# GpSimd's power for the next block's norm moved from slot 43 to slot 45, the normalisations of x from slots 45-48 to 46-49

## What is computed

```python
x = x + layernorm(attention(layernorm(x)))
x = x + layernorm(ffn(layernorm(x)))
```

## Time and profile before

| | us |
|---|---|
| median of 3 runs | 2466.63 (2465.53 to 2471.25) |
| the profiled execution, its own time | 2470.34 |
| its span, first to last instruction | 2468.6 |
| TensorE busy | 2360.2 (96% of the span) |
| VectorE busy | 1564.6 (63%) |
| ScalarE busy | 1399.9 (57%) |
| GpSimd busy | 659.3 (27%) |
| mean granted TensorE clock | 0.983 of 2.4 GHz |

### The profile page before, as it was taken

One profiled execution on the slowest core, in us unless ns is written; L12 is line 12 of the kernel. 1 busy time (PEld: TensorE's weight loads), 2 busy tenths in 40 slices (PEclk: granted clock), 3 DMA queues, 4 the chain that ended last, 5 costly groups with the idle time before them and its releaser, 6 DMA issues.

```text
span 2468.6 us, 38369 instructions
## 1 busy us (share of the span) xinstructions
PE 2360.2 (96%) x13020; PEld 1082.7 (44%) x13020; DVE 1564.6 (63%) x4343; ACT 1399.9 (57%) x3867; POOL 659.3 (27%) x923
## 2 busy tenths in 40 slices
PE   7589999999999999999999999999999999999988
PEld 3244444444444444444444444444443444444433
DVE  7857476665757657575665757656575765757542
ACT  4647456474755647466464755647466564755710
POOL 5412313122231312223132231312223132222312
PEclk9799999999999999999999999999999999999999
DMA  5010121201212020121201112020121202012000
GB/s 148 19 49 21 52 52 36 69 18 43 45 44 60 27 73 23 35 52 35 69 19 52 35 46 58 31 72 20 35 52 44 61 19 70 17 52 52 19 18 18
DMA packets 99523, 108.89 MB, mean 44 GB/s; under 512 B 22895, under 2 KB 73199, under 8 KB 99311
## 3 DMA queue, kind: packets, MB, share of 16 engines
q1 hardware_dynamic: 98462, 105.65, 16.1%
q10 hardware_dynamic: 864, 0.79, 0.1%
HBM read 38.49 MB, written 16.78 MB: 22 GB/s over the span
## 4 chain that ended last, share of the span: by engine, by line
PE 91%; DVE 4%; ACT 2%; POOL 2%; issue 1%; DMA 0%; ACTq 0%; POOLq 0%; DVEq 0%; SPq 0%
PE dense L376 65%; PE psO L579 7%; PE score L563 4%; PE psO L376 4%; PE low L546 3%; PE score L546 3%; DVE st_ln L826 1%; PE low L563 1%; POOL rs_ln L1188 1%; PE low L382 1%; PE low L471 1%; ACT arena L768 1%; PE score L471 1%; POOL arena L1321 1%; PE score L382 1%
## 5 line engine op out<-in xcount | busy, mean ns | idle before, releaser
L376 PE MATMUL dense<-arena,wgu 128*128 128x512 f16 x3872 | 920.1, 379 | 1.0 <-DVE arena L929 1.0
L376 PE MATMUL dense<-wdn,arena 128*128 128x512 f16 x2112 | 540.4, 382 | 2.6 <-POOL arena L1258 2.6
L376 PEld LDWEIGHTS dense<-arena,wgu 128*128 128x128 f16 x3872 | 369.5, 97 | 393.7 <-issue 7.6
L768 ACT ACTIVATE arena<-score 128x512 f32<-128x512 f32 (+3 forms) x720 | 300.2, 437 | 228.5 <-PE score L563 188.3
L1129 DVE CUSTOM_DVE_ANT_0 low<-low,mmax 128x128 f32<-128x128 f32 (+3 forms) x672 | 278.3, 435 | 229.8 <-PE low L546 226.9
L1258 POOL TENSOR_TENSOR arena<-late,arena 128x512 f16<-128x512 f32 x176 | 203.5, 1156 | 820.6 <-DVE arena L963 610.1
L684 ACT ACTIVATE low<-low,ncol 128x128 f32<-128x128 f32 (+3 forms) x672 | 299.8, 446 | 129.1 <-DVE ncol L1129 122.4
L684 ACT ACTIVATE score<-score,ncol 128x384 f32<-128x384 f32 x352 | 214.3, 609 | 139.9 <-DVE ncol L1129 139.6
L376 PEld LDWEIGHTS dense<-wdn,arena 128*128 128x128 f16 x2112 | 200.5, 98 | 185.7 <-issue 12.5
L1129 DVE CUSTOM_DVE_ANT_0 score<-score,mmax 128x384 f32<-128x384 f32 x352 | 214.3, 649 | 76.8 <-PE score L546 75.9
L1321 POOL TENSOR_SCALAR_AFFINE_SELECT arena<-arena 128x512 f32<-128x512 f32 x240 | 157.6, 657 | 279.0 <-ACT arena L768 278.9
(11 more groups left out here) (181 smaller groups left out, 2919.4 us busy)
## 6 DMA issues: line engine op xcount, KB each, us to landing
qst<-arena SPq DMA_DIRECT2D x384, 64.0 KB, 2.0
kst<-arena SPq DMA_DIRECT2D x186, 128.0 KB, 2.6
xin<-x SPq DMA_DIRECT2D x16, 1024.0 KB, 5.1
late<-x SPq DMA_DIRECT2D x64, 256.0 KB, 2.8
out<-late SPq DMA_DIRECT2D x64, 256.0 KB, 2.0
qst<-mrow SPq DMA_DIRECT2D x96, 8.0 KB, 1.9
wgu<-wo_t SPq DMA_DIRECT2D x1, 1024.0 KB, 13.0
wgu<-wq_down SPq DMA_DIRECT2D x1, 768.0 KB, 4.3
```

The lines of the kernel that those rows point to most:

```text
L376: ins = nc.tensor.matmul(dst, w, a, start=first and k == 0, stop=last and k == len(tt) - 1)
L768: nc.scalar.activation(prob_of(e // HG)[:, e % HG, 0:wide], st_bank(e)[:, 0:wide], ACT.Exp, scale=1.0 / S_SCORE).then_inc(sem["exp"], 1)
```

## The change

The power for the next block's norm is issued by GpSimd in slot 45 instead of slot 43, behind the place where a slot's mask stands and ahead of the feed-forward part's work of that slot. GpSimd's order becomes: mask 4 (42), mask 5 (44), power ln1 (45), power lo 0 (45), mask 6 (46), addition 0 (47), mask 7 (48). The four normalisations of x stand in slots 46 to 49 instead of 45 to 48, so that on VectorE the first comes behind the norm of output tile 0 and the fourth behind the moments of output tile 1. The moments of x stay in slot 43. No instruction is added or removed.

```diff
-LN1_SLOT = 43
+LN1_SLOT, LN1_POWER, LN1_NORM = 43, 45, 46
...
-                    if nxt and LN1_SLOT + 2 <= slot < LN1_SLOT + 2 + NT:
-                        i = slot - LN1_SLOT - 2
+                    if nxt and LN1_NORM <= slot < LN1_NORM + NT:
+                        i = slot - LN1_NORM
                         dve.wait_ge(sem["rs"], val("rs", t, n_ln1))
                         normalise("ln1", xin[:, i, :], xin[:, i, :], i).then_inc(sem["ln1"], 1)
...
                     for e in exp_tiles:
                         if e % HG == 1 and e > 1:
                             keep_causal(e // HG - 1)
+                    if nxt and slot == LN1_POWER:
+                        power(t, "ln1", n_y)
                     if ffn:
                         for m in range(MI):
                             if slot == up_done(m, 1) + 2:
...
                                 power(t, "lo", n_y + i + 1, i, i + 1)
-                    if nxt and slot == LN1_SLOT:
-                        power(t, "ln1", n_y)
```

## The result

The changed kernel takes 2435.27 us (median of 4 runs, 2434.26 to 2437.07), against 2468.94 for the kernel before (median of 4 runs, 2465.53 to 2474.2): a ratio of 0.9869, 95% interval 0.9856 to 0.9881. The forecast was 2436. The profiled execution took 2435.92 us with a span of 2434.2, so 34.4 us less than before on either count. That pair flatters the change: before and after were executed again beside the experiments, and there the kernel before took 2467.1 to 2467.4 (medians of 7 to 19 executions) and the changed one 2436.2, so the gain between medians is nearer 31 to 32 us.

What follows compares the result with a forecast made beforehand. TensorE is the bound, pausing for GpSimd's masks queued behind a norm power that waits for VectorE. 19.2 + 5.3 + 9.4 = 33.9 us off the profiled 2470.34 gives 2436, range 2430 to 2450.

Steps and rivals of the forecast that it cites:

- Mask 5 runs before values 5 is due: GpSimd, slot 44: causal mask of stage 5 ends 1.7 us before TensorE's probability-times-V products (values 5) want it; their wait goes.
- Mask 6 is late next: GpSimd, slot 46: stage-6 mask queued behind two powers; pause of 2.6 us becomes 1.3, gaining 1.37 us a block, 19.2 total.
- Mask 7 just fits: GpSimd, slot 48: stage-7 mask ends 0.16 us before TensorE wants values 7, so it costs nothing.
- rival 2: 8% chance: mask 7 becomes the wait, making values 7 0.9 us late in 14 blocks, 2448 us.
- rivals 3 to 5: In order: pause at values 6 hidden, 2418, 5%; VectorE's moments delayed, slower, 2474, 2%; little gained, 2449 to 2453, 3%.
- The normalisations of x cost nothing: VectorE, slots 46 to 49: the later normalisations cost nothing; should their cover fail, at most 0.5 us a block.
- Block 0: First block, mask 5 behind a weight unit: values 5 3.9 us sooner, with clock 5.3 us taken (bounds 3.9 and 5.9).
- Clock: Blocks 1 to 14: the halved pause brings fewer TensorE clock drops; 9.4 of 11.4 us lost is won back.
- rival 1: 20% chance: clock goes on falling at values 6; 2445 us if half the blocks drop as now, 2454 if all 14.
- The first case's own range: Main case, 62%: 2431 to 2441 us, from 0.95 to 1.37 us a block and clock losses 0 to 4.
- The total wait at L579: TensorE's total wait at the probability-times-V products for GpSimd's mask: some 22 us, the longest near 1.7.

Runs made afterwards that it cites:

- Experiment 3: Changed kernel with the normalisations of x starting in slot 45 again, the power left in slot 45: 2441.53 us, run again 2442.19 us.
- experiment 5: Changed kernel plus one or two unused extra GpSimd powers behind ln1's power in blocks 1 to 14: 2443.26 us with one, 2466.23 us with two.
- experiment 6: Changed kernel with powers ln1 and lo 0 in slot 46 behind mask 6, addition 0 in slot 48 behind mask 7: 2418.87 us.
- experiment 1: Changed kernel with power ln1 back in slot 43, normalisations left in slots 46 to 49: 2467.63 us, ratio 1.0006 to the kernel before.
- experiment 4: Changed kernel with power and normalisations of blocks 1 to 14 put back, change kept in block 0 alone: 2462.61 us, beside 2467.09 for the kernel before.

## Why the prediction was right

The forecast was 2436 and the time 2435.27. Counted from the medians the forecast was a gain of 30.2, against 31 to 32 measured. By its steps:

- *Mask 5 runs before values 5 is due.* Right. It runs 0.47 after values 4 for 0.85 (0.46 and 0.84 had been taken from the last block), and the wait at values 5 is gone. The mask was to be stretched beside VectorE's split, by what the Trainium skill has in SBUF — State Buffer, "Who interferes with whom", and nothing else was; the trace agrees: 0.85 for the mask beside the usual 0.63, and VectorE's L970 takes 0.69 with the mask beside it and without.
- *Mask 6 is late next.* Right: values 6 6.75 after values 4 was forecast, 6.72 is in the trace, so 1.41 and not 1.37 a block, 19.7 us. Both unstretched durations, L1022's 0.16 and the power's 0.55, came as the last block had them. Experiment 3 shows the second is owed to the later normalisations, the one part of the change that isn't the order on GpSimd; experiments 5 and 6 show that this queue alone sets values 6.
- *Mask 7 just fits.* Right, with 0.14 to spare where 0.16 was worked out; rival 2 did not come. Nor did rivals 3 to 5: values 6 does wait, L1022 starts 5.28 after values 4 (5.26 before), and the 14 pauses are shorter by 1.41 with no clock lost in them.
- *The normalisations of x cost nothing.* Right; with them alone the time is that of the kernel before (experiment 1).
- *Block 0.* 5.3 forecast, 5.3 in the traces, 4.5 with that block alone changed (experiment 4). The number is right by a path that was partly wrong. The sum had 3.9 at values 5 and 1.4 for the clock; the trace has 2.8 at values 5 and 2.5 behind it. The low clock came already at values 4 (1.51 there), so the transposes L403 took 1.06 and not 0.60 and ended 2.9 after values 4 and not 1.8, and the weight unit and mask 5 behind it came later by as much; the clock was up again by values 5. That the two misses cancel is luck.
- *Clock.* 9.4 forecast. In blocks 1 to 14 all of it came back, 12.2 where 11.4 was the bound, since the loss per drop was up to 1.6 in the periods and 1.42 had been taken from one block. Against it stand 2.2 lost in block 16 and 0.6 at the start, neither of which the sum had; they differ from execution to execution. The net of 9.4 was met by terms that cancel, which is luck; that the shorter pause would bring the clock back was the mechanism, and it held. Of rival 1 the runs show the limit: no drop after 1.19 and 1.69, six in 14 after 2.66. Its price is written wrongly: 2 + 7 x 1.42 is 11.9; seven drops less the 2 us left over in the sum are 7.9, so 2444 and not 2445.
- *The first case's own range.* 2431 comes out only when the whole 11.4 of the clock is taken off the median of 2466.6, though 3.7 had just been said to be missing there. With the bounds named, the profiled execution gives 2434 to 2444. The measured time lies in both.

The total wait at L579 was put at 22 us and is 24.1, of which 7.2 is block 0's.

## What to carry to other kernels

On an engine that works in order, an instruction that waits for a third engine costs nothing by its wait alone, but holds up what is queued behind it: put short work on which the critical engine waits ahead of it, and follow the queue on until every such piece stands first, since the pause moves to the next one (here from mask 5 to mask 6; mask 7 was put first together with mask 6 in experiment 6, so its share is not shown alone). Look for an iteration of the same kernel that lacks the suspected work: the last block gave the durations of the forecast for blocks 1 to 14 to some hundredths; block 0, which had no such counterpart, was where the path went wrong. And a pause of the critical engine has two prices, its length and the clock after it; here the second was 12.2 of the 31.9 us won in blocks 1 to 14.

## What had not been expected of the hardware

- After the same pause the clock falls in some blocks and not in others: with pauses of 2.60 to 2.66 us that repeat to a hundredth, seven of 14 blocks lose it in the kernel before and six in experiments 1, 4 and 5 (two extra powers). It does not look like plain chance: experiments 1 and 4 lose it in the same six blocks (1, 2, 5, 7, 10, 13) and experiment 5 in five of these and block 4, while the kernel before has 1, 3, 6, 8, 9, 11 and 14. What picks the block stays open. With 1.69 none did.
- A drop costs 1.3 to 1.6 us. In block 8 of the kernel before, after a pause of 2.91, it cost 2.75; three other kernels have 2.91 to 2.98 there and no drop.
- In block 0 TensorE waits 2.9 us for VectorE (L1008) just ahead of values 4, before and after the change. In the changed kernel the clock is low behind it (values 4 takes 1.51), in the kernel before it is not (1.06).
- A GpSimd power of 128x1 took 0.79 beside a VectorE normalisation of 128x512 and 0.55 alone, the whole of it on TensorE's path, 0.24 a block.
